# A four-layer graph kernel on one core: joined seams and last layer reordered, ramps, masks and counts moved around the third layer

## The chip, the cores and the metric

The kernel runs on one core of a Trainium2 chip. The core has five engines with a queue of instructions each: TensorE (PE in the profile; PEld is its weight load), VectorE (DVE), ScalarE (ACT), GpSimd (POOL) and SyncE (SP), which issues all DMAs here. Engines wait for each other through semaphores: an instruction that waits holds up everything behind it on its own engine. The metric is the device time of one launch in microseconds (us). The kernel before takes 433.39 us (median of 3 runs, 433.2 to 433.7).

## The reference

Four graph layers over N = 1354 nodes with D = 256 features, fp32, and an adjacency matrix `adj` whose nonzero entries are weights. Before each layer x is normalised and clipped, and each layer's result is added to x. Cut to what is computed:

```python
h = relu(layernorm(x)); x += softmax(q @ k.T / 16 + adj + adj) @ v          # layer 0, q, k, v from h
h = relu(layernorm(x)); x += L1(h)                                          # layer 1
h = relu(layernorm(x)); x += (adj != 0) @ (h @ W + b) / deg[:, None]        # layer 2, deg = column sums of adj != 0
h = relu(layernorm(x)); x += L3(h)                                          # layer 3

# L1
attn_a, attn_b = sigmoid([adj @ h, h] @ Wa.T + ba), sigmoid([adj @ h, h] @ Wb.T + bb)
g = h @ W_sa
e = where(adj != 0, exp(-leaky_relu(g @ a_left + (g @ a_right).T, 0.01)), 0)
x_a = e / (e.sum(1) + 1e-5) @ g
x_b = adj @ (h @ W_gcnb) + b_gcnb
return sigmoid(attn_a * x_a + attn_b * x_b)

# L3
S = adj + eye; g = h @ W
att = softmax(where(S > 0, g @ U @ g.T, -inf))
return (S * att) @ g
```

## The kernel before, in words

All of `adj` (transposed) and x stay in SBUF. The 1354 nodes are 11 blocks of 128 rows (the last has 74). The N x N work is tiled as 3 column groups (512, 512 and 330 columns) times 11 row blocks: tile n = 11 * group + block, n from 0 to 32. Within a group each tile adds to sums that stay in PSUM, in one bank for each of the group's 4, 4 or 3 blocks of 128 columns; the group is finished by VectorE, which reads those banks. PSUM has 8 banks.

Products that need accuracy are split in two parts with the suffixes `hi` and `lo`: ScalarE writes the rounded value (`hi`), VectorE or GpSimd the remainder (`lo`), and TensorE multiplies hi by hi, lo by hi and hi by lo. So each tile makes a round through TensorE, VectorE, ScalarE, VectorE and TensorE again. The order on each engine is written out by hand, in loops over a step number; semaphores enforce the data's order and the reuse of buffers. There is no scheduler.

- Layer 0 to layer 1 (the first seam). `project_h` and `project_g` (TensorE, L1375) project the blocks; ScalarE's `g_hi`, `h1_hi` and VectorE's `g_lo` (L924), `h1_lo` (L936) split them. For tile n of layer 1, `adj_hi` (ScalarE, L610, writes `mid_hi`) and `adj_lo` (VectorE L1066 for even n, GpSimd L397 for odd n, writes `mid_lo`) split the adjacency, and TensorE's `aggregate_b` (L1458, L1459 with hi parts, L1463 with the lo part) uses them. `lay_left` (TensorE L1564) lays out a row vector for all partitions.
- Layer 1, the joined loop over k from 8 to 40. TensorE runs `aggregate_b(k)` and `aggregate_a(k - 8)`. For the latter VectorE makes `mask(n)` (L1073) and `ramp(n)` (L1081), ScalarE `exp1(n)` (L619, L620, writes `p_hi`), VectorE `e_lo_part(n)` (L1088, writes `p_lo`). `join` (L1114 to L1124) and `add_gated` end a group. From k = 27 on, ScalarE's `z2` and `h2_hi` (L465, L473) and VectorE's `h2_lo` (L1154) prepare layer 2 beside it.
- Layer 2. `mask_2(n)` (VectorE L1143) writes a mask of zeros and ones for each tile, and `aggregate2(n)` (TensorE L1670, L1671) adds up. `count_b(group)` (VectorE L1225, L1229) follows a group's sums, and `y_out` (ScalarE L723), `turn_y` (TensorE L1682), `yT_out` (ScalarE L729), `project2` (TensorE L1698) and `out2` (VectorE L1237, then statistics L813, L818) end each block. `plus_eye` (GpSimd L420) adds the unit matrix to the adjacency. `norm` (GpSimd L360) makes the normalising factors of a group of blocks, `z` (ScalarE L451) applies them, `turn` (TensorE L1345) transposes a block, `h_hi` (L479) and `h_lo` (L829) split it, and `make_t(group)` (TensorE L293 to L295), `t_hi_part` (L487) and `t_lo_part` (VectorE L838, writes `mid_lo`) make the left operand of layer 3's scores.
- Layer 3. At step s TensorE computes `score(s)` (L293 to L295), VectorE `add3(s)` (L1283), `running(s)` (L891, a minimum over tiles), and after the group's minimum is known `shift(s - 13)` (L899), ScalarE `exp3` (L791), VectorE `times_s(s - 14)` (L1291, writes `w_ring`, 3 tiles deep), TensorE `aggregate3(s - 15)` (L1736). `turn_max` (L1436), `top` (VectorE L870, writes `mx`) and `spread_max` (L1445) bring the minimum to all partitions. GpSimd's `add_total` (L436) sums the weights, `add_up` (TensorE L1746) reduces them over partitions, and `out3(group)` (VectorE L1299, L1303) divides, adds to x and releases the output DMAs.

Of the kernel before, what the change touches and what calls it, by code (L numbers as in the profile page):

```python
# [5 lines left out]
ALU = mybir.AluOpType  # L6
# [21 lines left out]
SLOTS3 = 18  # L28
RING = 3
# [52 lines left out]
def graph_layers_kernel(nc, x, adjT, wq, wk, wvT, wsa, wgcn, w2, w3, w3T, u3T, asa, cols, rws, eye, out):  # L82
    with ExitStack() as ctx:
# [192 lines left out]
        eye_add, w_set, tot_add, tot_mm = sem("eye_add"), sem("w_set"), sem("tot_add"), sem("tot_mm")  # L276
# [73 lines left out]
        def _(pool):  # L350
# [72 lines left out]
            norm(2, 2)  # L423
            for b in range(NB):
                plus_eye(b)
            for gi in range(NG):
                norm(3, gi)
# [15 lines left out]
        def _(act):  # L443
# [286 lines left out]

            tanh(2)
# [5 lines left out]
            for b in range(8, NB):  # L737
                z2(b)
                h2_hi(b)
# [6 lines left out]
            for b in range(4):  # L746
                yT_out(b + 4)
                z(b, 3)
            h_hi(0, 3)
            h_hi(1, 3)  # L750
            z(4, 3)
            h_hi(2, 3)
            z(5, 3)
            h_hi(3, 3)
            z(6, 3)
            z(7, 3)
            for b in range(8, NB):
                y_out(b)
            t_hi_part(0, 1)


            for s in range(NB):
# [14 lines left out]
                if s == 9:  # L777
                    values(8, 1)
                    t_hi_part(2, 1)
                if s == 10:  # L780
                    values(9, 1)
                    values(10, 1)

            def exp3(n):

                gi, j = n // NB, n % NB
                act.wait_ge(s_sub[1], n + 1)
                if j == 0:
# [9 lines left out]
        def _(dve):  # L798
# [346 lines left out]
            def h2_lo(b):  # L1145

                r = rows(b)
                dve.wait_ge(zd, 2 * NB + b + 1)
# [10 lines left out]
            for b in blocks(2):  # L1159
                stats(b, 1)  # L1160
            for b in blocks(2):
                aggr(b, 1)
            g_lo(7)
            h1_lo(4)
            adj_lo(0)
            h1_lo(5)
# [13 lines left out]
            g_lo(10)  # L1180
            h1_lo(8)
            h1_lo(9)
            adj_lo(6)
            h1_lo(10)
            adj_lo(8)
            for k in range(LEAD, NT + LEAD):
# [8 lines left out]
                if m + 3 < NT:  # L1195
                    mask(m + 3)
                    ramp(m + 3)
# [15 lines left out]
                if 34 <= k < NT + LEAD:  # L1213
                    h2_lo(k - 34)
# [27 lines left out]
            h2_lo(7)  # L1242
            mask_2(8)
            mask_2(9)
            join(2)
            for n in range(10, 13):
                mask_2(n)
# [5 lines left out]
            for n in range(13, 19):  # L1253
                mask_2(n)
            for b in range(8, NB):
                h2_lo(b)
                mask_2(2 * b + 3)
                mask_2(2 * b + 4)
            for n in range(25, NT):
# [3 lines left out]
            for gi in range(2):  # L1263
                count_b(gi)
                for b in blocks(gi):
                    out2(b)
            for b in range(4):
                h_lo(b, 3)
# [3 lines left out]
            def add3(n):  # L1272
# [47 lines left out]
            for s in range(NB, NT + LAG - 1):  # L1320
                for gi in range(NG):
                    if s == NB * gi + 12:
                        top(gi, 1, ALU.min)
                    if gi < 2 and s == NB * gi + 26:
                        out3(gi)
                if s < NT:
                    add3(s)
                if 13 <= s < NT + 13:
                    shift(s - 13, 1)
# [8 lines left out]
        def _(pe):  # L1338
# [87 lines left out]
            def turn_max(gi, a):  # L1426
# [207 lines left out]
            project_h(10)  # L1634
# [189 lines left out]
```

## Time and profile before

| | us |
|---|---|
| median of 3 runs (lowest, highest) | 433.39 (433.2, 433.7) |
| the profiled execution's own time | 433.35 |
| its span on the chip | 431.6 |
| TensorE busy | 397.9 (92%), 2534 matmuls |
| VectorE busy | 333.6 (77%) |
| ScalarE busy | 222.6 (52%) |
| GpSimd busy | 94.9 (22%) |
| mean granted TensorE clock | 0.994 of full |

The span runs from the first to the last instruction; 1.75 us of the execution's time lie outside it. The profile lists for a group of instructions its busy time and the idle time of the engine just before it, with what ended that idle time. Matmuls are pipelined, so the profile's busy time of TensorE includes the overlap of one matmul with the next.

```profile
PE   7999999999999889999999898998889899989795
PEld 6787778989899778999999798986667788988674
DVE  4899799899875757898998889654637778778872
PEclk9999999999999999999999999999999999999989
```

The first two and the fourth line show TensorE, its weight load and its granted clock in 40 slices of 10.8 us, in tenths; the third shows VectorE.

### The profile page before, as it was taken

How to read it: one execution, taken by the hardware profiler on the slowest of the kernel's cores; microseconds unless marked ns; L12 is line 12 of the kernel's file. 1: busy time of each engine (PE TensorE's matmuls, PEld its weight loads, DVE VectorE, ACT ScalarE, POOL GpSimd, SP SyncE). 2: the span in 40 equal slices, each digit the busy share in tenths (PEclk: the TensorE clock that was granted, in tenths of full speed). 3: DMA queues.
4: the chain of work that ended last, by engine and by line, in shares of the span. 5: the costliest groups of instructions: out<-in, count | busy, mean ns of one | idle time of the engine just before them, and what ended most of it. 6: DMA issues, size and time to landing. Idle time of an engine off the chain costs nothing.

```text
span 431.6 us, 7349 instructions
## 1 busy us (share of the span) xinstructions
PE 397.9 (92%) x2534; PEld 357.0 (83%) x2534; DVE 333.6 (77%) x766; ACT 222.6 (52%) x457; POOL 94.9 (22%) x105
## 2 busy tenths in 40 slices
PE   7999999999999889999999898998889899989795
PEld 6787778989899778999999798986667788988674
DVE  4899799899875757898998889654637778778872
ACT  1443899974885647786686864244223212212230
POOL 1180000001010314331230109110010033424461
PEclk9999999999999999999999999999999999999989
DMA  8992000000000001000000000000000000010010
GB/s 254 373 374 74 2 0 2 2 0 2 0 2 2 1 2 49 2 2 2 1 2 2 2 0 2 2 0 2 0 2 1 2 1 0 2 49 2 12 38 31
DMA packets 10300, 13.96 MB, mean 32 GB/s; under 512 B 644, under 2 KB 7192, under 8 KB 10264
## 3 DMA queue, kind: packets, MB, share of 16 engines
q1 hardware_dynamic: 10264, 13.49, 9.2%
q8 instruction: 21, 0.34, 0.3%
q14 instruction: 15, 0.12, 0.1%
HBM read 12.10 MB, written 1.39 MB: 31 GB/s over the span
## 4 chain that ended last, share of the span: by engine, by line
PE 64%; DVE 19%; issue 8%; ACT 5%; DMA 1%; POOL 1%; DVEq 0%; SPq 0%; ACTq 0%; POOLq 0%
PE ps L1736 12%; PE ps L1463 8%; PE ps L1458 8%; PE ps L1459 7%; PE ps L293 6%; PE ps L295 5%; PE ps L294 5%; PE ps L1375 4%; PE ps L1698 2%; DVE m_sb L891 2%; DVE x_stats L813 2%; DVE s_sb L861 1%; DMA s_sb<-in_wk_dram 1%; DVE p_lo L905 1%; PE ps L1345 1%
## 5 line engine op out<-in xcount | busy, mean ns | idle before, releaser
L1458 PE MATMUL ps<-v_hi,p_hi 128*128 128x258 f32 (+3 forms) x242 | 64.5, 297 | 1.1 <-DVE x_sb L917 0.7
L1736 PE MATMUL ps<-v,w_ring 128*128 128x256 f32 (+3 forms) x242 | 57.5, 387 | 4.8 <-DVE x_sb L1303 3.2
L1459 PE MATMUL ps<-v_lo,p_hi 128*128 128x258 f32 (+3 forms) x242 | 61.1, 282 | 0.0
L1736 PEld LDWEIGHTS ps<-v,w_ring 128*128 128x128 f32 (+3 forms) x242 | 45.0, 190 | 13.0 <-issue 3.7
L360 POOL TENSOR_TENSOR mr_all<-mr_all,mhalf 128x4 f32<-128x4 f32 (+1 forms) x12 | 12.4, 1032 | 177.8 <-DVE mr_all L823 177.8
L1458 PEld LDWEIGHTS ps<-v_hi,p_hi 128*128 128x128 f32 (+3 forms) x242 | 44.6, 184 | 3.5 <-ACT p_hi L502 1.6
L436 POOL TENSOR_TENSOR total<-total,s_sb 128x512 f32<-128x512 f32 (+3 forms) x27 | 30.8, 1142 | 67.0 <-DVE w_ring L1291 67.0
L1459 PEld LDWEIGHTS ps<-v_lo,p_hi 128*128 128x128 f32 (+3 forms) x242 | 44.7, 185 | 0.5
L1463 PE MATMUL ps<-v_hi,p_lo 128*128 128x258 f32 (+3 forms) x242 | 40.5, 285 | 3.4 <-DVE p_lo L1088 1.7
L791 ACT ACTIVATE s_sb<-s_sb 128x512 f32<-128x512 f32 (+3 forms) x30 | 17.3, 576 | 48.9 <-DVE s_sb L899 48.9
L899 DVE TENSOR_TENSOR s_sb<-s_sb,ps 128x512 f32<-128x512 f32 (+3 forms) x63 | 38.5, 612 | 0.0
L1463 PEld LDWEIGHTS ps<-v_hi,p_lo 128*128 128x128 f32 (+3 forms) x242 | 32.5, 185 | 5.0 <-DVE p_lo L905 2.5
L397 POOL TENSOR_TENSOR mid_lo<-adjT_sb,mid_hi 128x512 fp32r<-128x512 f32 (+2 forms) x16 | 20.9, 1305 | 56.7 <-ACT mid_hi L610 56.7
L891 DVE TENSOR_TENSOR m_sb<-m_sb,s_sb 128x512 f32<-128x512 f32 (+3 forms) x51 | 32.7, 640 | 0.6
L1458 PE MATMUL ps<-big_hi,mid_hi 128*128 128x258 f32 (+3 forms) x121 | 31.3, 290 | 1.9 <-ACT mid_hi L610 1.9
L1283 DVE SCALAR_TENSOR_TENSOR s_sb<-adjT_sb,ps 128x512 f32<-128x512 f32 (+3 forms) x30 | 18.5, 616 | 18.7 <-PE ps L295 18.7
L293 PE MATMUL ps<-mid_hi,v_hi 128*128 128x512 f32 (+3 forms) x66 | 28.5, 432 | 2.4 <-DVE mid_lo L838 1.4
L1459 PE MATMUL ps<-big_lo,mid_hi 128*128 128x258 f32 (+3 forms) x121 | 30.3, 282 | 0.0
L619 ACT ACTIVATE p_hi<-s_sb,minus_r 128x512 fp32r<-128x512 f32 (+3 forms) x33 | 22.2, 673 | 14.2 <-DVE s_sb L1081 7.1
L1081 DVE SCALAR_TENSOR_TENSOR s_sb<-s_sb,sx 128x512 f32<-128x512 f32 (+3 forms) x33 | 28.4, 860 | 1.2
L293 PE MATMUL ps<-mid_hi,big_hi 128*128 128x512 f32 (+3 forms) x66 | 25.3, 383 | 0.8 <-DVE mid_lo L842 0.8
L502 ACT ACTIVATE p_hi<-s_sb 128x512 fp32r<-128x512 f32 (+3 forms) x33 | 19.1, 578 | 12.9 <-DVE s_sb L899 12.6
(227 smaller groups left out, 1062.9 us busy)
## 6 DMA issues: line engine op xcount, KB each, us to landing
adjT_sb<-in_adjT_dram SPq DMA_DIRECT2D x1, 2816.0 KB, 16.5
adjT_sb<-in_adjT_dram SPq DMA_DIRECT2D x3, 768.0 KB, 10.3
adjT_sb<-in_adjT_dram SPq DMA_DIRECT2D x1, 1815.0 KB, 20.9
out_dram<-x_sb SPq DMA_DIRECT2D x10, 128.0 KB
x_sb<-in_x_dram SPq DMA_DIRECT2D x2, 512.0 KB, 5.2
adjT_sb<-in_adjT_dram SPq DMA_DIRECT2D x1, 512.0 KB, 11.4
rows_sb<-in_rows_dram SPq DMA_DIRECT2D x1, 385.0 KB, 10.9
s_sb<-in_wq_dram SPq DMA_DIRECT2D x1, 256.0 KB, 4.0
```

Of the source, the lines that this page charges most:

```text
L293: eng.matmul(out_ap, lhs[0], rhs[0], start=first, stop=False)
L294: eng.matmul(out_ap, lhs[0], rhs[1], start=False, stop=False)
L295: return eng.matmul(out_ap, lhs[1], rhs[0], start=False, stop=last)
L436: pool.tensor_tensor(r, r, slot3(n), ALU.add).then_inc(tot_add, 1)
L619: act.activation(ring(p_hi, n), sum1(n), ACT.Exp, bias=bias, scale=SLOPE - 1.0).then_inc(e_hi, 1)
L891: dve.tensor_tensor(m, m, mine(n), op).then_inc(s_max[a], 1)
L899: dve.tensor_tensor(mine(n), mine(n), ps[0:rows(j), bank, 0:CW[gi]], ALU.subtract).then_inc(s_sub[a], 1)
L1081: dve.scalar_tensor_tensor(out=sum1(n), in0=left[0:rows(j), gi, 0:CW[gi]], scalar=sx[0:rows(j), j, 0:1], in1=sum1(n), op0=ALU.add, op1=ALU ...
L1458: pe.matmul(out_ap, left_[0][0:k, n % RING, mine], right_[0][0:k, j, 0:cols_], start=(j == 0), stop=False)
L1459: pe.matmul(out_ap, left_[0][0:k, n % RING, mine], right_[1][0:k, j, 0:cols_], start=False, stop=False)
L1463: ins = pe.matmul(ps[0:rows(b), banks[b % PER], 0:cols_], left_[1][0:k, n % RING, mine], right_[0][0:k, j, 0:cols_], start=False, stop=(j ...
L1736: ins = pe.matmul(ps[0:rows(b), B3.sums[b % PER], 0:D], w_ring[0:k, n % RING, mine], v3[0:k, j, :], start=(j == 0), stop=(j == NB - 1))
```

## The change

It reorders instructions on all engines, moves some PSUM banks, and touches no tile size. The parts:

- First seam. GpSimd's `adj_lo(1)` goes ahead of `sides(1)`; TensorE's `aggregate_b(0)` and `aggregate_b(7)` go ahead of `lay_left(1)` and `lay_left(2)`; ScalarE's `adj_hi(6)`, `(7)` and `(8)` each go one or two blocks' copies ahead; VectorE's `g_lo(7)` and `h1_lo(4)`, `h1_lo(5)` go in between the statistics.
- Ramps. At k = 22 and k = 27 VectorE makes two masks and ramps where it made one, so that from there on it is one and then two tiles further ahead; `h2_lo` starts at k = 36, not 34, and `z2`, `h2_hi` from block 4 on one step later.
- Around layer 2. VectorE makes the `z` of blocks 8 to 10 itself. `count_b(0)` stands ahead of the last masks and the weight splits, `h_lo(0)` and `h_lo(1)` of layer 3 between the `out2`, and `t_lo_part(0)` ahead of `count_b(2)`. TensorE's turns of blocks 0 to 3 alternate over banks 4 and 1 and start three tiles earlier, and `make_t(0)` goes ahead of the last two `aggregate2`. GpSimd's `norm(3, 0)` goes ahead of `plus_eye`.
- Layer 3. `out2` goes ahead of `add3`, and `project2` of blocks 8 to 10 gets banks of its own. `shift`, `times_s` and `aggregate3` follow the scores 11, 12 and 13 steps later in the first group and 12, 13 and 14 in the others (before: 13, 14, 15); `values` of blocks 8 to 10 move behind. The last group sums into banks 4, 5 and 7, not into those of group 1; all totals go to columns of bank 3; the last `add_up` stands inside the last tile, and each block of the last group is finished alone.

The diff, cut to its core:

```diff
+LAG3 = 14
+def ramps_at(k):
+    first = k - LEAD + 3 + (k > 22) + (k > 27)
+    return range(first, min(first + (2 if k in (22, 27) else 1), NT))
+
+def shift_step(n):
+    return n + (11 if n < NB else 12)
+
+def tiles_at(s, after):
+    return [n for n in range(NT) if shift_step(n) + after == s]
...
-TURNED = {0: [2, 4, 1, 0] + [2, 4] * 3 + [2], 1: [3] * NB, 3: [4] * 4 + [3] * 4 + [3, 0, 3]}
+TURNED = {0: [2, 4, 1, 0] + [2, 4] * 3 + [2], 1: [3] * NB, 3: [4, 1, 4, 1] + [3] * 4 + [3, 0, 3]}
+SUMS3 = [[0, 1, 2, 3], [0, 1, 2, 3], [4, 5, 7]]
+TOTALS_BANK = 3
-Y_BANKS = [4, 5, 4, 5, 0, 1, 0, 1, 0, 0, 0]
-P2_BANKS = [6, 7, 6, 7, 2, 3, 2, 3, 7, 7, 7]
+Y_BANKS = [4, 5, 4, 5] + [0] * 7
+P2_BANKS = [6, 7, 6, 7, 2, 3, 2, 3, 6, 7, 6]
...
 # GpSimd
+            norm(3, 0)
             for b in range(NB):
                 plus_eye(b)
...
 # ScalarE
+            for b in range(8, NB):
+                values(b, 1)
+                exp3(b - 8)
+            for n in range(3, NT):
                 exp3(n)
...
 # VectorE, joined loop
-                if m + 3 < NT:
-                    mask(m + 3)
-                    ramp(m + 3)
+                for n in ramps_at(k):
+                    mask(n)
+                    ramp(n)
...
-                if 34 <= k < NT + LEAD:
-                    h2_lo(k - 34)
+                if 36 <= k < NT + LEAD:
+                    h2_lo(k - 36)
...
 # VectorE, end of layer 2
+            for b in range(4):
+                out2(b)
+            mask_2(NT - 1)
+            count_b(1)
+            for b in range(4, 8):
+                out2(b)
+                if b == 6:
+                    h_lo(0, 3)
+                if b == 7:
+                    h_lo(1, 3)
+            h_lo(2, 3)
+            h_lo(3, 3)
+            t_lo_part(0, 1)
             count_b(2)
...
 # VectorE, layer 3 (steps 13 on)
+                if s == 24:
+                    times_s(11)
+                    out3(0)
+                if s == 37:
+                    out3(1)
                 if s < NT:
                     add3(s)
+                if s < 22:
+                    for n in tiles_at(s, 0):
+                        shift(n, 1)
                 if s < NT:
                     running(s, 1, ALU.min)
-                if s >= 14:
-                    times_s(s - 14)
+                for n in tiles_at(s, 1):
+                    if n != 11:
+                        times_s(n)
+                if s >= 22:
+                    for n in tiles_at(s, 0):
+                        shift(n, 1)
...
 # TensorE, layer 3
+                if n == 2 * NB:
+                    pe.wait_ge(s_add[1], NT)
+                    pe.wait_ge(s_sub[1], 2 * NB)
                 for b in blocks(gi):
+                    if n == NB:
+                        pe.wait_ge(x_add[3], b - PER + 1)
...
+                    if n == NT - 1:
+                        ins.then_inc(last_sum, 1)
+                        if b == 2 * PER:
+                            add_up(2)
```

Three places, in the order in which the engine's instructions stand (line numbers of each kernel's own; `x2` is two in a row). The first is ScalarE at the first seam: `mid_hi` is `adj_hi`, `big_hi` is `g_hi`, `sx` and `v_hi` are `h1_hi` of a block, `p_hi` and `s_sb` are `exp1`. Before:

```order
L526 ACTIVATE big_hi<-ps 128x258
L610 ACTIVATE mid_hi<-adjT_sb 128x512
L526 ACTIVATE big_hi<-ps 74x258
L538 ACTIVATE sx<-ps 128x4
L540 ACTIVATE v_hi<-ps 128x256
L619 ACTIVATE p_hi<-s_sb,minus_r 128x512
L620 ACTIVATE s_sb<-s_sb,minus_r 128x512
L538 ACTIVATE sx<-ps 128x4
L540 ACTIVATE v_hi<-ps 128x256
L610 ACTIVATE mid_hi<-adjT_sb 128x512
```

After:

```order
L544 ACTIVATE big_hi<-ps 128x258
L628 ACTIVATE mid_hi<-adjT_sb 128x512 x2
L544 ACTIVATE big_hi<-ps 74x258
L556 ACTIVATE sx<-ps 128x4
L558 ACTIVATE v_hi<-ps 128x256
L628 ACTIVATE mid_hi<-adjT_sb 128x512
L637 ACTIVATE p_hi<-s_sb,minus_r 128x512
L638 ACTIVATE s_sb<-s_sb,minus_r 128x512
L556 ACTIVATE sx<-ps 128x4
L558 ACTIVATE v_hi<-ps 128x256
```

`adj_hi(6)` stood behind two blocks' `h1_hi` and an `exp1`; it now stands beside `adj_hi(5)`, and `adj_hi(7)` ahead of `exp1(1)`.

The second is VectorE between the masks of layer 2 and its first `out2`: `s_masks` and `p_hi` are masks, `z_buf` the new normalisation, `big_lo` is `h2_lo`, `wb_lo` and `wa_lo` are weight splits, `rb` and the `x_sb` behind it are `count_b(0)`. Before:

```order
L1154 SCALAR_TENSOR_TENSOR big_lo<-z_buf,big_hi 74x256
L1143 TENSOR_SCALAR s_masks<-adjT_sb 128x330 x9
L1143 TENSOR_SCALAR p_hi<-adjT_sb 74x330
L803 TENSOR_TENSOR wb_lo<-raw_b,wb_hi 128x2x256
L803 TENSOR_TENSOR wa_lo<-gram,wa_hi 128x2x256
L1225 TENSOR_TENSOR rb<-ps,rdeg 128x4
L1229 SCALAR_TENSOR_TENSOR x_sb<-rows_sb,rb,x_sb 128x256 x4
L1237 SCALAR_TENSOR_TENSOR x_sb<-ps,rdeg,x_sb 128x256
```

After:

```order
L1174 TENSOR_SCALAR z_buf<-x_sb,mr_all 128x256
L1182 SCALAR_TENSOR_TENSOR big_lo<-z_buf,big_hi 74x256
L1167 TENSOR_SCALAR s_masks<-adjT_sb 128x512
L1167 TENSOR_SCALAR s_masks<-adjT_sb 74x512
L1167 TENSOR_SCALAR s_masks<-adjT_sb 128x330 x6
L1254 TENSOR_TENSOR rb<-ps,rdeg 128x4
L1258 SCALAR_TENSOR_TENSOR x_sb<-rows_sb,rb,x_sb 128x256 x4
L1167 TENSOR_SCALAR s_masks<-adjT_sb 128x330 x4
L827 TENSOR_TENSOR wb_lo<-raw_b,wb_hi 128x2x256
L827 TENSOR_TENSOR wa_lo<-gram,wa_hi 128x2x256
L1266 SCALAR_TENSOR_TENSOR x_sb<-ps,rdeg,x_sb 128x256
```

`count_b(0)` now has four masks and both weight splits behind it that stood ahead of it.

The third is TensorE at the very end: `w_ring` is `aggregate3` of the last tile, `ones,total` is `add_up(2)`. Before:

```order
L1736 MATMUL ps<-v,w_ring 74x256
L1736 MATMUL ps<-v,w_ring 128x256 x2
L1736 MATMUL ps<-v,w_ring 74x256
L1746 MATMUL ps<-ones,total 128x1 x2
L1746 MATMUL ps<-ones,total 74x1
```

After:

```order
L1798 MATMUL ps<-v,w_ring 74x256
L1798 MATMUL ps<-v,w_ring 128x256
L1814 MATMUL ps<-ones,total 128x1 x2
L1814 MATMUL ps<-ones,total 74x1
L1798 MATMUL ps<-v,w_ring 128x256
L1798 MATMUL ps<-v,w_ring 74x256
```

The reduction of the totals now stands behind the first of the last tile's three blocks.

## Rows read from the trace of the kernel before

**Rows 1.** Stretches of the span: busy us (count) of each engine, clock.

```profile
core 0: us, PE busy (x) PEld busy (x) DVE busy (x) ACT busy (x) POOL busy (x), PEclk, DMA share, GB/s
...
198.00:250.00 52.00, 49.03 (x378) 46.45 (x377) 47.24 (x123) 40.29 (x89) 7.99 (x10) 1.00 0.01 2
409.50:412.90 3.40, 2.92 (x7) 2.23 (x8) 2.93 (x6) 1.39 (x3) 1.68 (x2) 0.50 0.46 154
```

**Rows 2.** TensorE's waits: total us, times, longest us.

```profile
PE ps L1736 <- DVE x_sb L1303: 3.2, 2, 2.1
PE ps L1345 <- ACT z_buf L451: 2.3, 2, 2.0
...
PE ps L1458 <- ACT mid_hi L610: 1.9, 2, 1.7
PE ps L1698 <- DVE x_sb L1237: 1.9, 2, 1.0
...
PE ps L1463 <- DVE p_lo L1088: 1.7, 3, 0.9
...
PE ps L1736 <- DVE w_ring L1291: 1.6, 1, 1.6
PE ps L293 <- DVE mid_lo L838: 1.4, 1, 1.4
PE ps L1463 <- DVE mid_lo L1066: 1.0, 2, 0.7
...
PE ps L1682 <- ACT h_mid L723: 0.9, 1, 0.9
...
PE ps L1375 <- DVE big_lo L924: 0.8, 1, 0.8
...
PE ps L1564 <- ACT sx L538: 0.7, 2, 0.4
...
PE ps L1445 <- DVE mx L870: 0.6, 1, 0.6
PE ps L1345 <- DVE v_lo L829: 0.6, 2, 0.3
PE ps L1670 <- DVE big_lo L1154: 0.5, 1, 0.5
```

**Rows 3.** TensorE in order of time: start us, length us.

```profile
167.27 0.28 PE L1458 MATMUL ps<-v_hi,p_hi 128*128 128x258 f32 x1
167.39 0.28 PE L1459 MATMUL ps<-v_lo,p_hi 128*128 128x258 f32 x1
...
418.82 7.07 PE L1736 MATMUL ps<-v,w_ring 128*74 128x256 f32 x32
```

**Rows 4.** Groups of VectorE between 165 and 250 us.

```profile
L1081 DVE SCALAR_TENSOR_TENSOR s_sb<-s_sb,sx 128x512 f32<-128x512 f32 (+3 forms) x30 | 24.7, 822 | 1.1
...
L1073 DVE TENSOR_SCALAR s_sb<-adjT_sb 128x512 f32<-128x512 f32 (+3 forms) x30 | 13.2, 440 | 0.0
```

**Rows 5.** VectorE in order of time, in the joined loop and behind layer 2.

```profile
228.48 0.16 DVE L1114 TENSOR_TENSOR rs<-ps,e_left 128x4 f32<-128x4 f32 x1 [1.46 <-PE ps L1463]
...
286.73 0.48 DVE L1237 SCALAR_TENSOR_TENSOR x_sb<-ps,rdeg,x_sb 128x256 f32<-128x256 f32 x1 [0.42 <-PE ps L1698]
...
288.09 0.42 DVE L829 SCALAR_TENSOR_TENSOR v_lo<-ps,v_hi 128x256 fp32r<-128x256 f32 x1
```

**Rows 6.** VectorE in the last group of layer 3.

```profile
411.95 0.48 DVE L899 TENSOR_TENSOR s_sb<-s_sb,ps 128x330 f32<-128x330 f32 x1
412.99 0.50 DVE L1291 TENSOR_TENSOR w_ring<-s_sb,adjT_sb 128x330 f32<-128x330 f32 x1 [0.55 <-ACT s_sb L791]
413.41 0.49 DVE L899 TENSOR_TENSOR s_sb<-s_sb,ps 128x330 f32<-128x330 f32 x1
...
426.40 0.29 DVE L1299 RECIPROCAL rinv<-ps 128x1 f32<-128x1 f32 x3 [3.61 <-PE ps L1746]
426.62 1.25 DVE L1303 SCALAR_TENSOR_TENSOR x_sb<-ps,rinv,x_sb 128x256 f32<-128x256 f32 x3
```

**Rows 7.** GpSimd's last addition to the totals.

```profile
422.88 0.88 POOL L436 TENSOR_TENSOR total<-total,s_sb 74x330 f32<-74x330 f32 x1 [0.44 <-DVE w_ring L1291]
```

More of the change, by code:

```diff
@@ L423, in _ @@
             norm(2, 2)
+            norm(3, 0)
             for b in range(NB):
                 plus_eye(b)
-            for gi in range(NG):
-                norm(3, gi)
+            norm(3, 1)
+            norm(3, 2)
             def add_total(n):
@@ L745, in _ @@
                 y_out(b)
-            for b in range(4):
-                yT_out(b + 4)
-                z(b, 3)
+            yT_out(4)
+            z(0, 3)
+            yT_out(5)
+            z(1, 3)
+            yT_out(6)
+            z(2, 3)
             h_hi(0, 3)
-            h_hi(1, 3)
+            yT_out(7)
+            z(3, 3)
+            for b in range(1, 4):
+                h_hi(b, 3)
             z(4, 3)
-            h_hi(2, 3)
             z(5, 3)
-            h_hi(3, 3)
+            t_hi_part(0, 1, (0,))
             z(6, 3)
+            t_hi_part(0, 1, (1,))
             z(7, 3)
@@ L1158, in _ @@
             add_out(2)
-            for b in blocks(2):
-                stats(b, 1)
+            g_lo(7)
+            stats(8, 1)
+            h1_lo(4)
+            stats(9, 1)
+            stats(10, 1)
+            h1_lo(5)
             for b in blocks(2):
                 aggr(b, 1)
-            g_lo(7)
-            h1_lo(4)
             adj_lo(0)
-            h1_lo(5)
             h1_lo(6)
@@ L1252, in _ @@
                 aggr(b, 2)
-            for n in range(13, 19):
+            for n in range(13, 20):
                 mask_2(n)
@@ L1256, in _ @@
                 h2_lo(b)
-                mask_2(2 * b + 3)
-                mask_2(2 * b + 4)
-            for n in range(25, NT):
+            for n in range(20, 28):
+                mask_2(n)
+            count_b(0)
+            for n in range(28, 32):
                 mask_2(n)
@@ L1319, in _ @@
                     t_lo_part(2, 1)
-            for s in range(NB, NT + LAG - 1):
-                for gi in range(NG):
-                    if s == NB * gi + 12:
-                        top(gi, 1, ALU.min)
-                    if gi < 2 and s == NB * gi + 26:
-                        out3(gi)
+            add3(11)
+            top(0, 1, ALU.min)
+            shift(0, 1)
+            shift(1, 1)
+            add3(12)
+            times_s(0)
+            running(12, 1, ALU.min)
+            for s in range(13, NT + LAG3 - 1):
+                for gi in range(1, NG):
+                    if s == NB * gi + (12 if gi == 1 else 11):
+                        top(gi, 1, ALU.min)
+                if s == 24:
[3 more added lines that the diff above has]
+                    out3(1)
                 if s < NT:
                     add3(s)
-                if 13 <= s < NT + 13:
-                    shift(s - 13, 1)
+                if s < 22:
+                    for n in tiles_at(s, 0):
+                        shift(n, 1)
                 if s < NT:
                     running(s, 1, ALU.min)
-                if s >= 14:
-                    times_s(s - 14)
+                for n in tiles_at(s, 1):
[4 more added lines that the diff above has]
+                        shift(n, 1)
             out3(2)
```

155 lines of the change are left out of this document (81 added, 74 removed).

## The prediction

> **What bounds the kernel now.** I read the busy shares first: TensorE is busy for 92% of the span, VectorE for 77%, the others for at most 52%. So TensorE's own work sets most of the time, and it is not changed: as many matmuls, of the same shapes. What can be won is its idle time. The second view is therefore the list of TensorE's waits [rows 2]; the largest are all short and each has another cause: the late `out3` (first row), the normalised z, a late `mid_hi`, `out2`, `p_lo`, `w_ring`. The third is stretches [rows 1]. In the joined loop (198 to 250 us) VectorE is busy for 47.24 us of 52.00 and TensorE for 49.03, so there both are nearly full and what VectorE does more of can be paid. In the last stretch of rows 1 TensorE's granted clock is 0.50: half of full, the 1.2 GHz level, with 7 matmuls in it, behind the longest wait of rows 2 (2.1 us, for `out3(1)`).
>
> What a wait costs is more than its bracket. Behind one, matmuls start every 0.12 us while each takes 0.28 [rows 3]: the pipeline refills, and the listed wait ends later than the loss began by 0.28 - 0.12 = 0.16. I count the bracket plus 0.16 for each wait that goes.
>
> The profiled execution took 433.35 us (span 431.6 and 1.75 outside it); the median of the runs is 433.39, so the sum is made against either.
>
> **First seam, 4.2 gained.** `adj_hi(6)` to `(8)` stand ahead of other copies: the wait for `mid_hi` (1.9 in two) goes. With `g_lo(7)` between the statistics that for `big_lo` (0.8 in one), and with `aggregate_b(0)` and `(7)` ahead of `lay_left` those for `sx` (0.7 in two) [rows 2]. 3.4 and 5 times 0.16 is 4.2. Nothing is added on any engine; GpSimd's tile 1 only changes place with `sides(1)`.
>
> **Joined loop, 0.5 lost.** The additional mask and ramp at k = 22 and at k = 27 are work brought forward, not more work: 0.440 + 0.822 = 1.26 us of VectorE each [rows 4]. But at k = 22 they stand ahead of the `mid_lo` of a tile that TensorE waits for already (1.0 in two, L1066 in rows 2), so there up to 1.26 is lost at once. The second falls near `join(1)`, in which VectorE itself waited 1.46 us for TensorE (the first of [rows 5]), and is hidden by that. Given back is `p_lo`: 1.7 in three [rows 2], 2.2 with the refills, since the ramp no longer stands between; also `h2_lo` begins two tiles later. If VectorE is the bound of the whole stretch nothing is given back: 1.26 and a refill, -1.4. If TensorE is, both kinds of wait shrink and it is +1.7. I take -0.5, nearer the first, because 47.24 of 52.00 is nearly full.
>
> **Layer 2, 3.3 gained.** Gone are the waits for `mid_lo` of L838 (1.4), for `h_mid` (0.9), the short one for z (2.3 - 2.0 = 0.3), for `big_lo` of L1154 (0.5) and the two for `v_lo` (0.6) [rows 2]: 3.7, with 6 times 0.16 4.7. New is what `turn` of block 3 waits for in its bank: `h_lo(1)`, which VectorE makes behind `out2(7)`. Now the last `out2` starts at 286.73 and the first `h_lo` 1.36 later, and takes 0.42 [rows 5]; the statistics stand in that 1.36. So TensorE waits for about 1.0 where it had 0.6, and some 0.4 more on banks that turns share. 4.7 - 1.4 = 3.3. Its bounds: 4.7, and 1.6 if the two orders of `h_lo` and `out2` (1.36 + 0.42 each, less what hides) both stand in the way.
>
> **Start of layer 3, 4.3 gained.** `project2` of blocks 8 to 10 has banks of its own and `out2` stands ahead of `add3`: the two waits for L1237 (1.9) go. VectorE makes the z of blocks 8 to 10 as soon as it has the sums: the 2.0 for `z_buf` goes [rows 2]. 3.9 and 3 times 0.16 is 4.3 (rounded down). The bound below is 1.9: VectorE now has three 128 x 256 operations (some 0.45 each) more where ScalarE was free, so that `score` could wait for `add3`.
>
> **Layer 3, 5.9 gained.** The two waits for `out3` (3.2: L1303 in rows 2) go, since group 2 has other banks and group 1 waits block by block; `w_ring` (1.6) goes, as times_s of tile 11 stands ahead of `out3(0)`; `mx` (0.6) goes: 5.4, with 4 refills 6.0. With the idle of 2.1 us its half clock goes as well: 7 matmuls started every 0.43 instead of 0.22 us (7.07 / 32, rows 3): 7 x 0.21 and the fall's edge, 1.6. At the end three reciprocals (0.29) and three divisions (1.25) stand behind the last matmul [rows 6]; only the last block's stay, about 0.5, and the rest runs beside TensorE: 1.0. Against it stand 0.8 for two small waits (`spread_max` and the first `aggregate3` come sooner behind `top` and `values`), and the drain. In the last group after the last score, a tile goes through shift, exp, `times_s` in turn on VectorE and ScalarE. `shift` starts at 411.95, `times_s` 1.04 later behind an exponential, the next shift 0.42 behind that [rows 6]: 1.46 a tile if, with the shorter distance, each `times_s` needs the exponential of the shift just made. TensorE needs 6 matmuls of 0.22, 1.3. Over 8 tiles that is 8 x 0.16 = 1.3 lost. GpSimd's last addition takes 0.88 [rows 7] and stands before `add_up(2)` beside only one block's matmuls (2 x 0.22): 0.5. All losses: 0.8 + 1.4 + 0.5 = 2.7 (the drain as 1.4, with an edge), and 6.0 + 1.6 + 1.0 - 2.7 = 5.9.
>
> Sum: 4.2 - 0.5 + 3.3 + 4.3 + 5.9 = 17.2. 433.35 - 17.2 = 416.1 us.
>
> Two rules speak to this. Rows 1 show one fall to half clock, and only behind the longest idle of TensorE. The Trainium skill, "TensorE: Matmul & The Clock Gate", section "A second HAM failure mode: psum-queue depth-cycling", has a kernel whose TensorE idles very shortly between groups of matmuls, and whose gate swings between its levels for that. By that rule the drain, with a gap at each tile, would fall again; by the row it stays at full clock, since nothing of 2 us is left. No row of before shows such a fall behind short gaps. It is a rival below.
>
> **Rivals.**
> (1) VectorE paces from the seam to the end of the joined loop. For it: 47.24 of 52.00 [rows 1]. Against it: its 1.46 of idle in `join(1)` [rows 5], and that TensorE waited for it only 2.7 us (1.7 + 1.0) there. Then the seam's 4.2 is no gain for TensorE but becomes waits for `mid_lo` and `p_lo`: 416.1 + 4.2 = 420.3.
> (2) No new wait. The drain is hidden by the 3-deep `w_ring`, the turns find their banks free, the loop gains 1.7. 416.1 - 2.7 - 1.4 + 0.1 = 412.
> (3) The clock falls in the drain. TensorE idles at every tile there. One fall cost 1.6 here (7 matmuls at 0.43); two or three give 3.2 to 4.8 more: about 420. This is where the page's rule leads.
> (4) Slower. The half clock holds through the last group, because the drain's gaps never let the engine reach what it needs to recover. At 0.21 for each matmul (above) the change is slower from 17.2 / 0.21 = 82 matmuls at half clock on. The group's 66 `aggregate3` (11 tiles of six) and some 24 of group 1's that run beside its first scores make 90, 19 us: 416.1 + 19 = 435. The trace speaks against it: only 7 matmuls fell behind an idle of 2.1 us, and recovery came by itself.
> (5) The change does not do what it says: the waits of rows 2 move to the next instruction of another engine, as nearly all of them are short and each has a second producer not far behind. At half the sum, 425.
>
> **How the numbers follow.** The forecast has 0.5, rival 1 0.15, rival 2 0.12, rival 3 0.08, rival 5 0.11, rival 4 0.04. The forecast alone is 413.5 to 418.5, from the bounds of layer 2 (+1.4, -1.7) and the loop (+2.2, -1.0) that hardly all fall on one side. The range of 8 in 10 takes rivals 1, 2 and 3: 411.5 to 422.5. This kernel's measurement tells a change from none at about 0.2%, 0.9 us. Faster by more than that is 0.95 by these cases (rival 4 has 0.04, of which a third would leave it about where it was, and so would a hundredth of the others), same 0.02, slower 0.03.
>
> **What the profile after would show.** Right: no wait of TensorE for `mid_hi`, `out3`'s `x_sb` or `z_buf` over 0.5 us; `aggregate_b(8)`, the last of the seam, some 4 us earlier; granted clock 1.00 in the last group; a wait of `turn` for `v_lo` of about 1 us; in the drain VectorE's `times_s` waiting for the exponential just before it, and TensorE for `w_ring` by 0.1 to 0.3 at each tile. Joined loop: a wait for `mid_lo` near k = 23. Wrong: if between the seam's end and the end of the joined loop the lead of 4 us is lost again (rival 1), if the clock reads under 1.00 anywhere behind 400 us (rivals 3, 4), or if the sum of TensorE's waits falls by less than half.

## The result and the profile after

| | before | after |
|---|---|---|
| median of the runs (lowest to highest), us | 433.54 (433.2 to 435.63, 4 runs) | 415.07 (414.89 to 415.58, 4 runs) |
| ratio, 95% interval | | 0.9572, 0.9545 to 0.9599 |
| profiled execution, its span | 433.35, 431.6 | 415.22, 413.4 |
| TensorE busy | 397.9 (92%) | 394.8 (95%) |
| VectorE busy | 333.6 (77%) | 329.1 (80%) |
| mean granted clock | 0.994 | 0.996 |

The change makes the kernel 18.5 us faster (18.1 between the two profiled executions); 17.2 were forecast, inside a range of 411.5 to 422.5. The number of matmuls is the same, 2534; TensorE's idle time went, and with it the half clock at 409.5 us. (The mean clock of 0.996 comes from the 4 us behind the last matmul: 0.62 of full there.) These are all its waits of 0.2 us or more that are left, as total, times and longest (us):

```profile
PE ps L1536 <- DVE m_sb L964: 2.0, 1, 2.0
PE ps L1517 <- DVE mid_lo L1090: 1.8, 2, 1.4
PE ps L1517 <- DVE p_lo L929: 1.7, 4, 0.6
PE ps L309 <- DVE s_sb L1322: 1.0, 1, 1.0
PE ps L1401 <- DVE v_lo L853: 1.0, 1, 1.0
PE ps L309 <- DVE v_lo L875: 0.9, 1, 0.9
PE ps L1517 <- POOL mid_lo L413: 0.9, 1, 0.9
PE ps L1490 <- DVE m_sb L915: 0.8, 2, 0.6
PE ps L1798 <- DVE w_ring L1330: 0.8, 2, 0.5
PE ps L309 <- DVE mid_lo L866: 0.8, 1, 0.8
PE ps L1512 <- DVE x_sb L941: 0.7, 1, 0.7
PE ps L1798 <- issue: 0.5, 1, 0.5
PE ps L1517 <- DVE p_lo L1112: 0.4, 2, 0.2
PE ps L1814 <- POOL total L453: 0.3, 1, 0.3
PE ps L1512 <- ACT p_hi L520: 0.3, 1, 0.3
PE ps L1408 <- ACT gram L728: 0.2, 1, 0.2
PE ps L1512 <- DVE s_sb L1148: 0.2, 1, 0.2
```

Against [rows 2]: the waits for `out3` (3.2), `z_buf` (2.3), `mid_hi` (1.9), `out2` (1.9), T's `mid_lo` of L838 (1.4), `h_mid` (0.9), `big_lo` (0.8 and 0.5), `sx` (0.7) and `mx` (0.6) are gone; `p_lo` fell from 1.7 to 0.4. The `w_ring` wait of 1.6 is gone too, but for 0.5 that the list puts down to issue at the same matmul; the 0.8 in two of `w_ring` are new. Larger than before are `mid_lo` of the adjacency (L1090, 1.8 where L1066 had 1.0), `mid_lo` from GpSimd inside the seam (L413, 0.9 where L397 had 0.3), and the turn's `v_lo` (1.0 in one where it had 0.6 in two). The whole list of before, of which [rows 2] is a part, adds up to 28.2 us, this one to 14.3.

How much each stage gave is read by the same matmul in both traces: the first of `aggregate_b(8)` (end of the seam), of `aggregate2` (end of the joined loop) and of the last layer's scores. Before:

```profile
165.83 0.28 PE L1458 MATMUL ps<-big_hi,mid_hi 128*128 128x258 f32 x1
...
250.16 0.28 PE L1670 MATMUL ps<-big_hi,s_masks 128*128 128x258 f32 x1
...
297.34 0.50 PE L293 MATMUL ps<-mid_hi,v_hi 128*128 128x512 f32 x1 [1.41 <-DVE mid_lo L838]
```

After:

```profile
161.29 0.37 PE L1512 MATMUL ps<-big_hi,mid_hi 128*128 128x258 f32 x1
...
245.03 0.28 PE L1724 MATMUL ps<-big_hi,s_masks 128*128 128x258 f32 x1
...
288.01 0.50 PE L309 MATMUL ps<-mid_hi,v_hi 128*128 128x512 f32 x1
```

The leads are 4.54, 5.13 and 9.33 us, and 18.1 at the end (0.3 of the first was there before the seam). As many matmuls (972, 1618 and 1928) stand ahead of the three marks in both traces, so the leads compare like with like:

| stage | forecast | measured |
|---|---|---|
| first seam | 4.2 | 4.2 |
| joined loop | -0.5 | 0.6 |
| layer 2 | 3.3 | 4.2 |
| layer 3, its start and the rest | 4.3 + 5.9 = 10.2 | 8.8 |

The drain, VectorE in the last group (start, length, what it waited for), answers to [rows 6]:

```profile
403.06 0.51 DVE L1330 TENSOR_TENSOR w_ring<-s_sb,adjT_sb 128x330 f32<-128x330 f32 x1 [0.55 <-ACT s_sb L808]
403.48 0.49 DVE L923 TENSOR_TENSOR s_sb<-s_sb,ps 128x330 f32<-128x330 f32 x1
404.52 0.50 DVE L1330 TENSOR_TENSOR w_ring<-s_sb,adjT_sb 128x330 f32<-128x330 f32 x1 [0.55 <-ACT s_sb L808]
...
408.26 0.18 DVE L1338 RECIPROCAL rinv<-ps 128x3 f32<-128x3 f32 x1 [1.79 <-PE ps L1814]
408.48 1.26 DVE L1344 SCALAR_TENSOR_TENSOR x_sb<-ps,rinv,x_sb 128x256 f32<-128x256 f32 x3
```

`times_s` follows `times_s` by 404.52 - 403.06 = 1.46 us, and each waits 0.55 for the exponential of the shift just made. TensorE goes at that pace, not at its own:

```profile
394.88 12.35 PE L1798 MATMUL ps<-v,w_ring 128*128 128x256 f32 x50 [0.29 <-DVE w_ring L1330]
407.49 0.74 PE L1814 MATMUL ps<-ones,total 128*128 128x1 f32 x6 [0.26 <-POOL total L453]
408.09 1.11 PE L1798 MATMUL ps<-v,w_ring 74*128 74x256 f32 x4
```

12.35 / 50 is 0.247 us a matmul; [rows 3] had 7.07 / 32 = 0.221. The loss does not show as idle time: TensorE is read as busy for 6.00 of 6.00 us below, and in each tile of six matmuls two start 0.27 and 0.32 behind the one before instead of 0.22. It shows in the waits of the weight load, over the whole of the last layer:

```profile
PEld ps L1798 <- DVE w_ring L1330: 4.5, 11, 0.8
```

The granted clock (last but two of the columns) is whole in it:

```profile
400.00:406.00 6.00, 6.00 (x26) 4.01 (x25) 3.67 (x9) 2.04 (x5) 3.72 (x5) 1.00 0.01 3
406.00:408.00 2.00, 1.74 (x10) 0.96 (x9) 0.47 (x1) 0.00 (x0) 0.88 (x1) 1.00 0.00 0
408.00:409.30 1.30, 1.20 (x7) 0.65 (x7) 1.00 (x4) 0.00 (x0) 0.00 (x0) 1.00 0.00 0
```

### The profile page after: what moved, and what is told of

The parts are those of the page before. It is cut to its first block, busy times and chain, and to the rows that moved or that the text cites. A ratio compares the mean times of both kernels' runs of the same rounds, so it can differ in the third digit from the quotient of the medians.

```text
span 413.4 us, 7338 instructions
## 1 busy us (share of the span) xinstructions
PE 394.8 (95%) x2534; PEld 355.2 (86%) x2534; DVE 329.1 (80%) x761; ACT 220.7 (53%) x454; POOL 89.5 (22%) x105
## 4 chain that ended last, share of the span: by engine, by line
PE 72%; DVE 17%; issue 6%; ACT 2%; POOL 1%; DVEq 0%; POOLq 0%; ACTq 0%
PE ps L1798 9%; PE ps L1517 9%; PE ps L1512 8%; PE ps L1513 8%; PE ps L309 6%; PE ps L311 6%; PE ps L310 6%; PE ps L1431 4%; PE ps L1725 3%; PE ps L1724 3%; PE ps L1754 2%; DVE m_sb L915 2%; PE ps L1536 2%; DVE s_sb L885 2%; DVE p_lo L929 1%
## 5 line engine op out<-in xcount | busy, mean ns | idle before, releaser
L1798 PEld LDWEIGHTS ps<-v,w_ring 128*128 128x128 f32 (+3 forms) x242 | 43.2, 186 | 11.1 <-DVE w_ring L1330 4.5
L376 POOL TENSOR_TENSOR mr_all<-mr_all,mhalf 128x4 f32<-128x4 f32 (+1 forms) x12 | 13.3, 1106 | 173.6 <-DVE mr_all L847 173.6
L413 POOL TENSOR_TENSOR mid_lo<-adjT_sb,mid_hi 128x512 fp32r<-128x512 f32 (+2 forms) x16 | 20.6, 1289 | 51.4 <-ACT mid_hi L628 51.4
L1105 DVE SCALAR_TENSOR_TENSOR s_sb<-s_sb,sx 128x512 f32<-128x512 f32 (+3 forms) x33 | 26.0, 789 | 1.2
L1322 DVE SCALAR_TENSOR_TENSOR s_sb<-adjT_sb,ps 128x512 f32<-128x512 f32 (+3 forms) x30 | 18.5, 616 | 10.3 <-PE ps L311 10.0
```

The lines of the kernel that those rows point to most:

```text
L1105: dve.scalar_tensor_tensor(out=sum1(n), in0=left[0:rows(j), gi, 0:CW[gi]], scalar=sx[0:rows(j), j, 0:1], in1=sum1(n), op0=ALU.add, op1=ALU ...
L1798: ins = pe.matmul(ps[0:rows(b), SUMS3[gi][b % PER], 0:D], w_ring[0:k, n % RING, mine], v3[0:k, j, :], start=(j == 0), stop=(j == NB - 1))
```

## The experiments

Ten kernels were run: one is the kernel before with one part of the change, the others the changed kernel with one part undone or up to three things more. Medians are compared with 415.07 for the changed kernel; its runs lay within 0.7 us, and the kernel before, measured again beside the experiments, had medians from 433.0 to 433.9. So differences of medians under about 1 us are read in the trace. There too something has to be taken off: by 10 us, before any edited instruction, the profiled executions are already between 0.4 us behind the changed kernel's and 0.95 ahead of it, for instance by 1.08 us of waiting for the first weights (`in_wk_dram`) in one of them. A gain is the lead behind the edit minus the lead ahead of it.

**The seam alone, in the kernel before.**

```diff
# GpSimd: adj_lo(1) ahead of sides(1); ScalarE: adj_hi(6), (7), (8) ahead
+            g_lo(7)
+            stats(8, 1)
+            h1_lo(4)
...
+            aggregate_b(0)
             lay_left(1)
-            aggregate_b(0)
```

> The kernel before with the edits of the first seam alone. Theory (TensorE paces behind the seam too): the seam's idle (4.2 us by the two traces, 4.2 in the prediction) goes and stays gone, 433.4 - 4.2 = 429.2. Rival (VectorE paces from the seam through the joined loop): the lead is lost by the end of the loop, 432 to 433.4, with longer waits of TensorE for p_lo and mid_lo between 165 and 250 us.

429.6 us (428.23 to 431.32), ratio to before 0.9898 (0.9862 to 0.9934), 4.3 us less than the 433.86 of the kernel before measured beside it; by the interval, 2.9 to 6.0. The trace is sharper: against the kernel before its TensorE leads by 1.04 us ahead of the seam, by 5.30 at `aggregate_b(8)`, 5.18 at the end of the joined loop and 5.21 at 409.9 us. So 4.3 are won and 4.2 stay. The seam's gain is no loan: TensorE's waits for `p_lo` (1.7 in three) and `mid_lo` (1.1 in two) in the loop are those of [rows 2]. VectorE doesn't pace the stretch as a whole, and rival 1 falls.

**The ramps back.**

```diff
-    first = k - LEAD + 3 + (k > 22) + (k > 27)
-    return range(first, min(first + (2 if k in (22, 27) else 1), NT))
+    first = k - LEAD + 3
+    return range(first, min(first + 1, NT))
```

> The changed kernel with one mask and one ramp at each step, as before; h2_lo, z2 and all else stay changed. Theory A (the prediction's price of the ramps, 1.4 at once and nothing given back by them): the wait for mid_lo of tile 24 shrinks from 1.4 us to about 0.5 and no other grows, 415.1 - 1.0 = 414.1. Theory B (the ramps are why TensorE's waits for p_lo behind 235 us went, from 1.7 in three to 0.4 in two): those waits come back, 1.3 and a refill, and the mid_lo wait shrinks by 1.0: 415.4 to 415.9, that is, no difference that can be measured, but another distribution of waits. If 417 or more, the ramps carry more than their waits.

415.1 us (414.75 to 415.61): no difference. Its waits:

```profile
PE ps L1517 <- DVE mid_lo L1090: 1.0, 2, 0.7
...
PE ps L1517 <- DVE p_lo L1112: 0.7, 3, 0.3
```

The additional mask and ramp at k = 22 do cost what they were priced at, at once: `mid_lo` 1.8 with them, 1.0 without, and the matmul that waits comes 0.78 us earlier (0.05 of it was there ahead of it). By the end of the loop 0.12 of the 0.78 is left; the rest is lost near step 40, in `p_lo` and between. Theory B.

**h2_lo back to step 34, ramps kept.**

```diff
-                if 36 <= k < NT + LEAD:
-                    h2_lo(k - 36)
+                if 34 <= k < NT + LEAD:
+                    h2_lo(k - 34)
# ScalarE: z2(4), h2_hi(4) at step 37 again
```

> The changed kernel with h2_lo from step 34 on again and z2, h2_hi of block 4 at step 37, as before. Undoing the ramps alone moved the time by nothing, so the loop's gain of 0.8 us must come from this part or from the lead out of the seam. Theory A (h2_lo's delay): the waits for p_lo behind 235 us come back to 1.7 in three, 1.3 more and up to two refills: 416.4 to 416.7. Theory B: no difference, 415.1.

415.12 us (415.02 to 415.66). `p_lo` waits rise to 1.1 in two, but not to 1.7, and the median doesn't move. In the trace a lead of 0.52 us ahead of the loop has shrunk to 0.12 at its end: 0.4 lost. Theory A's size was wrong.

**Both back.** The two diffs above together.

> The changed kernel with both parts of the joined loop undone: one ramp a step, and h2_lo, z2 and h2_hi as early as before. Either alone moved nothing (415.1 and 415.1), with TensorE's waits for p_lo of L1112 at 0.7 and 1.1 us instead of 0.4. Theory A (each covers the same waits, so one of the two is enough): p_lo comes back to 1.7 in three while mid_lo stays at 1.0 instead of 1.8; 415.1 + 0.8 = 415.9. Theory B (neither matters, the loop's 0.8 came from the lead out of the seam): 415.1 with p_lo at about 1.1.

415.58 us (415.0 to 416.27). The two waits are those of [rows 2] to a tenth:

```profile
PE ps L1513 <- DVE p_lo L1110: 1.7, 3, 0.9
...
PE ps L1513 <- DVE mid_lo L1088: 1.0, 2, 0.7
```

Between 9.9 us and the end of the loop its TensorE loses 0.7 us against the changed kernel in the trace (a lead of 0.42 becomes a lag of 0.30). The medians differ by 0.5, which is within the scatter of the runs. So the loop's 0.6 belongs to the two parts, which cover the same waits: with the later `h2_lo` alone nothing of it is lost, with the ramps alone 0.4.

**VectorE's adj_lo(24) ahead of its mask and ramp.**

```diff
+                if k == 23:
+                    adj_lo(k + 1)
                 for n in ramps_at(k):
```

> The changed kernel with VectorE's adj_lo(24) ahead of the mask and ramp of step 23. Theory (the wait of 1.4 us for mid_lo of tile 24 is the mask and ramp ahead of it, 0.42 + 0.75 less overlap 1.1): that wait falls to 0.3 or less, 415.1 - 1.1 = 414.0. Rival (VectorE has no slack up to the end of the loop, so that the gain comes back as longer waits for p_lo): 415.1, as the kernel without the additional ramps showed (its 0.8 at tile 24 was lost again down to 0.3).

414.5 us (414.4 to 415.67). Its profiled execution is 0.95 us ahead already at 8 us, before any edit, and 0.81 just ahead of the edited step. Tile 24's matmul comes 1.93 us earlier, so 1.12 is won there, and two tiles later the lead is 0.77: nothing of it is left. The `mid_lo` waits are 1.7 in three where they were 1.8 in two. Over these steps VectorE is full, and an operation put ahead makes another late. The rival held.

**out2 behind add3 again, banks kept.**

```diff
-                if 2 <= s < 5:
-                    out2(s + 6)
                 add3(s)
                 running(s, 1, ALU.min)
+                if 2 <= s < 5:
+                    out2(s + 6)
```

> The changed kernel with out2 of blocks 8 to 10 behind add3 and running of their step again; the banks of project2 stay changed. The prediction put the wait for z_buf (2.0) down to VectorE's making a z itself; but that z is layer 2's, and the z that was waited for is layer 3's of blocks 8 to 10, behind out2, its statistics and norm. Theory A (the order of out2 and add3 carries it): the two waits for out2 (1.9) stay short because of the banks, and the wait for z_buf comes back in part, since each out2 is 1.4 us later (0.69 and 0.69): 0.7 to 2.2 more, 415.8 to 417.3. Theory B (the banks carry all of it): 415.1, no wait for z_buf over 0.3.

419.0 us (417.28 to 419.07), 3.9 more: beyond theory A's upper end, and theory B falls. TensorE in order of time, at the turn of block 8:

```profile
307.23 0.44 PE L1401 MATMUL ps<-ident,z_buf 128*128 128x128 f32 x2 [2.05 <-ACT z_buf L468]
307.43 0.47 PE L309 MATMUL ps<-mid_hi,v_hi 128*128 128x512 f32 x1
```

and its stretches:

```profile
307.20:309.50 2.30, 2.27 (x8) 1.84 (x9) 0.00 (x0) 1.23 (x3) 0.00 (x0) 0.65 0.03 7
309.50:311.10 1.60, 1.60 (x9) 1.51 (x8) 0.00 (x0) 0.00 (x0) 0.00 (x0) 0.50 0.00 0
```

The whole `z_buf` wait of before is back (2.05), with waits for `out2` still gone. So the order carries the 2.0, and the 1.9 is left to the banks, which were not undone by themselves. On top the clock fell to half: by 311.4 us it is 3.90 behind, 2.29 by the wait (0.1 of it stood before) and 1.61 by the clock. The runs seem to show both cases: three at 419.0 to 419.1 (mean clock 0.991 or 0.992), two at 417.3 and 417.5 (0.996 and 0.999), and theory A's 417.3 is met by these two; only one of the slower was profiled.

**The last group's sums in banks 0 to 2 again.**

```diff
-SUMS3 = [[0, 1, 2, 3], [0, 1, 2, 3], [4, 5, 7]]
+SUMS3 = [[0, 1, 2, 3], [0, 1, 2, 3], [0, 1, 2]]
...
-                    pe.wait_ge(s_add[1], NT)
-                    pe.wait_ge(s_sub[1], 2 * NB)
+                    pe.wait_ge(x_add[3], 2 * PER)
```

> The changed kernel with the last group's sums in banks 0, 1 and 2 again, so that its first aggregate3 waits for out3(1). Theory: the wait of about 2 us returns and with it the granted clock's fall to half over some 7 matmuls: 2.1 + 0.16 + 1.5 = 3.7, less what w_ring is then ahead (VectorE and ScalarE run on during the wait, up to 3 tiles deep: the drain's 0.16 a tile is covered for the first tiles, 0.5): 418.3 to 418.8. Rival (the fall came from something else in that stretch): only 1.6 to 2.3 more, 417.0, with a granted clock of 1.00.

417.61 us (416.73 to 418.37), 2.5 more, where 3.2 to 3.7 were expected. The median lies between two pairs: 418.4 twice (mean clock 0.988), within what was expected, and 416.7 and 416.9 (0.992), near the rival's 417.0. The trace is of one of the slower. The wait is there, and the half clock behind it:

```profile
394.95 15.92 PE L1797 MATMUL ps<-v,w_ring 128*128 128x256 f32 x62 [2.67 <-DVE x_sb L1344]
```

```profile
388.00:392.20 4.20, 4.20 (x24) 3.61 (x22) 2.41 (x6) 2.07 (x4) 2.08 (x2) 1.00 0.00 0
394.90:398.00 3.10, 3.05 (x7) 2.35 (x8) 0.76 (x3) 0.48 (x1) 0.89 (x1) 0.50 0.39 130
398.00:401.00 3.00, 3.00 (x12) 2.22 (x11) 1.68 (x4) 0.48 (x1) 1.12 (x2) 0.73 0.00 0
```

It is 3.20 us behind at the wait (0.39 stood before) and 5.50 behind by 399.7, and then catches up to 3.2: VectorE ran its three `w_ring` tiles ahead and itself waited for TensorE,

```profile
397.96 0.50 DVE L1330 TENSOR_TENSOR w_ring<-s_sb,adjT_sb 128x330 f32<-128x330 f32 x1 [2.34 <-PE ps L1797]
...
400.19 0.50 DVE L1330 TENSOR_TENSOR w_ring<-s_sb,adjT_sb 128x330 f32<-128x330 f32 x1 [1.32 <-PE ps L1797]
```

so that the drain's slow round is hidden for the rest. What made the other two runs 1.6 faster is open; the fall did not come, came shorter, or lay elsewhere. A wait of TensorE is worth less than its length where it lets a slower chain behind it get ahead. This is what the forecast's drain term says from the other side.

**shift ahead of times_s in the drain.**

```diff
+                if s >= 36:
+                    for n in tiles_at(s, 0):
+                        shift(n, 1)
                 for n in tiles_at(s, 1):
                     if n != 11:
                         times_s(n)
```

> The changed kernel with shift of the next tile ahead of times_s from step 36 on, so that times_s no longer waits for the exponential of the shift just made. Theory (the round shift, exponential, times_s sets the drain's pace at 1.46 us a tile where TensorE's six matmuls need 1.30): the pace falls to 1.30, 8 x 0.16 = 1.3, and the wait for the totals (0.26 + 0.16) goes too, less 0.4 by which the first times_s is later: 415.1 - 1.2 = 413.9. Rival (TensorE is refilled at 1.46 for another reason, GpSimd's totals or the ring of three): no change, 415.1.

414.47 us (413.75 to 414.57). TensorE:

```profile
394.33 11.26 PE L1801 MATMUL ps<-v,w_ring 128*128 128x256 f32 x50 [0.29 <-DVE w_ring L1330]
405.98 0.74 PE L1817 MATMUL ps<-ones,total 128*128 128x1 f32 x6 [0.39 <-POOL total L453]
```

The same 50 matmuls take 11.26 us, not 12.35: 1.09 won, 0.225 us a matmul, its own pace. That is the theory's mechanism, shown. Not as expected, the totals' wait grew from 0.26 to 0.39. VectorE and GpSimd now work beside each other:

```profile
398.33 0.89 POOL L453 TENSOR_TENSOR total<-total,s_sb 128x330 f32<-128x330 f32 x1 [0.44 <-DVE w_ring L1330]
398.58 1.00 DVE L1330 TENSOR_TENSOR w_ring<-s_sb,adjT_sb 128x330 f32<-128x330 f32 x1
```

`times_s` takes 1.00 where it took 0.50, and of the last three additions the first takes 1.48, the others 0.96 and 0.88, where they took 0.89. The median moved by 0.6; in the trace TensorE's lead grows from 0.55 to 1.51 us, so 1.0 is won.

**out3(1) spread over four steps as well.**

```diff
-                if s == 37:
-                    out3(1)
...
+                if s == 37:
+                    out3(1, [])          # the reciprocals alone
+                if 38 <= s < 42:
+                    out3(1, [s - 34])    # one block
```

> The kernel with shift ahead of times_s from step 36 on, and in it out3(1) no longer in one piece (0.17 and 1.66 us) ahead of times_s but one block a step, behind times_s. Theory (the wait for w_ring near 394 us, 0.29 and its refill, is out3(1)): it goes, 414.5 - 0.4 = 414.1, and the totals' wait (0.4) stays. Rival (the spread blocks stand in the way of each shift by turns, 0.42 in a slack of 1.30 - 0.85): no gain, 414.5.

412.91 us (412.22 to 413.5), ratio to before 0.9523 (0.9502 to 0.9544): the fastest kernel of the study, 2.2 us under the changed one. The `w_ring` wait of 0.29 is gone, and so, not expected, is the one for the totals. Its profiled execution (413.5) is the slowest of its four: TensorE waited 1.08 us for the first weights, and up to the edit it is 0.48 behind the changed kernel. Its last matmuls are 1.7 us earlier, so the two repairs together won 2.2, as much as the medians say. That is 1.2 beyond the kernel with `shift` first, where 0.4 was expected; the two waits with their refills are 1.0 of it.

**The ramps at 27 and 30 in it.**

```diff
-    first = k - LEAD + 3 + (k > 22) + (k > 27)
+    first = k - LEAD + 3 + (k > 27) + (k > 30)
```

> The kernel with shift ahead of times_s and out3(1) spread over four steps, and in it the additional ramps at k = 27 and 30 instead of 22 and 27. Theory: the wait for mid_lo of tile 24 falls from 1.4 to 0.7 us as with the ramps undone, and p_lo stays at 0.4 since the ramps are ahead before step 36: 412.9 - 0.8 = 412.1. Rival (VectorE paces around step 30 too, behind join(1)): the wait comes back there as mid_lo or p_lo, 412.9.

413.85 us (413.23 to 414.89), no better. `mid_lo` waits are 1.7 in four instead of 1.8 in two: the 0.75 won at tile 24 is lost again behind it, and 0.6 more by the end of the loop. The rival held; no place was found in the loop where the work ahead is free.

## Why the prediction was right, point by point

- **First seam, 4.2.** Right in place and size, and the seam alone gives 4.3 on the chip. But the size is in part luck: the one wait of GpSimd's `mid_lo` in it grew from 0.3 to 0.9, which the sum had at nothing, so the other edits gave some 0.6 more than bracket plus 0.16 for each wait.
- **Joined loop, -0.5.** Wrong in sign, by 1.1 us. The price at k = 22 was right (0.78 at tile 24). What failed is the weight of what is given back: "nearer the first, because 47.24 of 52.00 is nearly full". The waits that go stand at the end of the loop (steps 38 to 40), the full steps in its middle (around 23), and the share over the whole stretch told nothing on either. `p_lo` fell from 1.7 to 0.4; the later `h2_lo` alone would have kept the gain, the ramps alone less than half of it.
- **Layer 2, 3.3.** The new wait is as forecast: `turn` waits 1.0 us for `v_lo` (L853). It is also the only one of 0.2 or more left in the layer, so the other 0.4, on shared banks, shows nowhere. With that wait in the sum, some 0.7 of the 4.2 stays unassigned. No kernel undoes a part of this layer: its gain is argued from the waits that are gone.
- **Start of layer 3, 4.3.** The sum was right: the first turn of the minimum (L1436, L1490) starts at 337.26 us before and at 321.58 after, and less the 18 matmuls of `values` that now come later (0.12 each, an estimate) and the 9.33 of lead, 4.2 were won there. But one of its reasons was not. The z that VectorE now makes is layer 2's; the z that TensorE waited 2.0 us for is layer 3's of blocks 8 to 10, behind `out2`, its statistics and `norm`. What removes it is `out2` ahead of `add3`, as the kernel with that order undone shows. The edit was also worth more than the term: the wait that it removes can take the clock down.
- **Layer 3, 5.9.** Mis-sized: with 4.3 at the start, 4.5 are left. The forecast waits for `out3` and `mx` went, the drain cost 1.1 (12.35 against 11.26 us, forecast 1.4), and the totals' wait was 0.3 with a refill (0.5). The term that was missing is `w_ring`: two new waits of 0.50 (at 367.32 us) and 0.29 (at 394.88), with two refills 1.1. TensorE waited for `out3(0)` and `out3(1)` before; now they stand, 1.8 us long, between two `times_s` that nothing covers. The spread `out3(1)` shows this for the second of them; for the first it is argued. With that 5.9 becomes 5.1; 0.6 stays in gaps that I can't assign. And the reason for the 1.6 was wrong: that wait stood at the layer's first `aggregate3`,

```profile
345.46 1.99 PE L1736 MATMUL ps<-v,w_ring 128*128 128x256 f32 x8 [1.60 <-DVE w_ring L1291]
```

  where `out3(0)`, which starts at 378.42 us, has no part. That `times_s` of tile 11 stands ahead of `out3(0)` can't have removed it; the shorter distance behind the scores may have, which no run separates.
- **The total.** It came within 1.0 us in part by luck: against the terms the joined loop gave 1.1 more, layer 2 0.9 more and layer 3 1.4 less, and 0.3 lay ahead of the seam.
- **The signs.** All of those for "right" that have a number came, but the 0.1 to 0.3 a tile shows in the spacing of the matmuls, not as waits. One of the signs for "wrong" lies at its edge: the sum of TensorE's waits fell from 28.2 to 14.3 us, by 49%, which is less than half. Some 8 of the 28.2 are waits that no part of the change was meant to remove.
- **Rivals.** 1 falls by the seam alone. 2 has a wrong sum: a loop that gains 1.7 instead of losing 0.5 takes off 2.2 more, so it stands at 409.8, not 412, and falls. 3 and 4 fall: the clock is 1.00 from 400 us to the last matmul, with some 0.16 us lost at each tile. By the rule on very short idles of TensorE between groups of matmuls (the Trainium skill, "TensorE: Matmul & The Clock Gate", "A second HAM failure mode: psum-queue depth-cycling") it would have swung; losses of about 0.16 us every 1.46 us, which the profile doesn't even show as idle, didn't do it here. Whether idles that it shows would, no run tells. 5 falls: the waits that are new or grew (`mid_lo`, `w_ring`, `v_lo`, the totals and three smaller ones) add up to some 3.5 us, against 17.4 that went.

## What to carry to other kernels

Count TensorE's waits with their refill, and then ask of each what chain ran ahead during it: the wait for `out3` hid a round of shift, exponential and product that is slower than TensorE, and removing it uncovered the round. Where one engine goes back and forth with another, issue the next tile's first step before this tile's last one. Read how full an engine is at the steps where the waits stand, not over the stage. And before a lead in a trace is put down to an edit, read it just ahead of the edit: here up to 1 us was there by 10 us.

## What the runs showed of the hardware

- Idle times of TensorE of about 2 us sometimes end in half clock and sometimes not. The one of 2.0 us at the start of layer 3 in the kernel before left the clock whole, as the stretch behind it shows,

```profile
318.70:321.00 2.30, 2.25 (x13) 2.00 (x14) 0.00 (x0) 1.26 (x3) 0.00 (x0) 1.00 0.00 0
```

  while its 2.1 us in the last group did not [rows 1]; one of 2.05 took it down in the profiled run of one kernel, and by times and mean clocks in three of its five. That fall cost 1.6 us, so this wait is worth 2.2 or 3.8, by the run; the fall behind the wait of 2.67 cost 2.3 (5.50 - 3.20) before the drain hid most of it.
- GpSimd's addition of 128 x 330 and VectorE's product of two 128 x 330 tiles in SBUF lengthen each other. Nearly apart, in the changed kernel's drain, they take 0.89 and 0.50 us. With `shift` first a product that starts during an addition takes 1.00, and the addition in which two products run takes 1.48.
